# High and low part of an activation in one TensorE product of 512 columns, in two layers of a feed-forward block

## The reference

```python
h = layernorm(x) * (1 + ca) + sa
x = x + ga * attn(h)      # chunked linear attention with a decayed state, 4 heads of 64, chunks of 64 tokens
h = layernorm(x) * (1 + cb) + sb
# feed-forward, ternary weights (-1, 0, 1), a scale for each output
h = silu((h @ w1.T) * s1) * ((h @ w2.T) * s2)     # 256 -> 1024, twice ("l1")
h = gelu((h @ h1.T) * s_h1)                       # 1024 -> 1024 ("l2")
h = gelu((h @ h2.T) * s_h2)                       # 1024 -> 1024 ("l3")
x = x + gb * ((h @ w3.T) * s3)                    # 1024 -> 256 ("y")
```

## Time and profile before

| | |
|---|---|
| median of 3 runs | 1745.33 us (1743.48 to 1747.3) |
| profiled execution, span from first to last instruction | 1742.3 us |
| mean granted TensorE clock | 0.991 of full speed |
| PE / PEld busy | 1716.0 us (98%) / 1651.6 us (95%) |
| DVE / ACT / POOL busy | 1115.4 us (64%) / 963.3 us (55%) / 593.5 us (34%) |

### The profile page before, as it was taken

How to read it: one execution, slowest core, us unless ns; L and a number is a source line. 1 busy time by engine, 2 the same in 40 slices (tenths; PEclk the granted TensorE clock), 3 DMA queues, 4 the chain that set the end, 5 groups by cost and what they waited for, 6 DMA issues and landing times.

```text
span 1742.3 us, 60528 instructions
## 1 busy us (share of the span) xinstructions
PE 1716.0 (98%) x25488; PEld 1651.6 (95%) x25488; DVE 1115.4 (64%) x3041; ACT 963.3 (55%) x2249; POOL 593.5 (34%) x694
## 2 busy tenths in 40 slices
PE   8799999999999999999999999999999999999999
PEld 5698999999999999999999999999999999999998
DVE  5677666666666666676666676666666666666432
ACT  4664555555555555555555555555555555565554
POOL 3544333343333343333243333243233243243101
PEclk8899999999999999999999999999999999999999
DMA  8101000000000000000000000000000000000000
GB/s 291 68 14 33 12 23 23 18 20 11 24 23 23 18 20 11 24 23 24 17 21 15 20 23 23 20 17 19 16 23 23 21 17 21 14 23 17 8 3 12
DMA packets 37356, 47.08 MB, mean 27 GB/s; under 512 B 9236, under 2 KB 29336, under 8 KB 37080
## 3 DMA queue, kind: packets, MB, share of 16 engines
q1 hardware_dynamic: 35088, 40.75, 8.4%
q10 hardware_dynamic: 1992, 2.38, 0.5%
HBM read 22.53 MB, written 8.39 MB: 18 GB/s over the span
## 4 chain that ended last, share of the span: by engine, by line
PE 93%; DVE 1%; issue 1%; POOL 1%; ACT 1%; DVEq 0%; POOLq 0%
PE mlp L1163 64%; PE mlp L1235 6%; PE solo L1163 3%; PE duo L1431 3%; PE solo L1304 3%; PE solo L1136 2%; PE duo L1352 1%; PE duo L1129 1%; PE duo L1420 1%; PE solo L1440 1%; PE duo L1124 1%; PE duo L1325 1%; PE solo L1146 1%; PE duo L1422 1%; PE duo L1316 1%
## 5 line engine op out<-in xcount | busy, mean ns | idle before, releaser
L1163 PE MATMUL mlp<-act_hi,w_hi 128*128 128x256 f32 x4096 | 968.0, 283 | 1.1 <-POOL act_lo L668 0.6
L1163 PE MATMUL mlp<-act_lo,w_hi 128*128 128x256 f32 x4096 | 945.2, 277 | 0.0
L1163 PEld LDWEIGHTS mlp<-act_hi,w_hi 128*128 128x128 f32 x4096 | 770.1, 188 | 9.8 <-POOL act_lo L668 1.3
L1163 PEld LDWEIGHTS mlp<-act_lo,w_hi 128*128 128x128 f32 x4096 | 770.4, 188 | 0.8
L805 ACT ACTIVATE full<-mlp,scale_sb 128x256 f32<-128x256 f32 x512 | 246.4, 481 | 553.7 <-PE mlp L1163 553.5
L895 DVE TENSOR_TENSOR act_lo<-full,act_hi 128x256 fp32r<-128x256 f32 x512 | 240.2, 469 | 321.7 <-ACT act_hi L806 319.1
L668 POOL TENSOR_TENSOR act_lo<-full,act_hi 128x256 fp32r<-128x256 f32 x256 | 186.6, 735 | 501.9 <-ACT act_hi L795 501.9
L806 ACT ACTIVATE act_hi<-mlp,scale_sb 128x256 fp32r<-128x256 f32 x512 | 242.6, 474 | 0.0
L1163 PE MATMUL mlp<-xh,w_hi 128*128 128x256 f32 x768 | 190.8, 286 | 3.5 <-issue 3.0
L1163 PE MATMUL mlp<-xl,w_hi 128*128 128x256 f32 x768 | 189.8, 282 | 0.0
L607 POOL TENSOR_TENSOR rstd<-ve,minus_half 128x2 f32<-128x2 f32 x64 | 49.1, 768 | 331.7 <-DVE ve L844 331.3
(11 more groups left out here) (179 smaller groups left out, 2679.9 us busy)
## 6 DMA issues: line engine op xcount, KB each, us to landing
w_raw<-in_wts SPq DMA_DIRECT2D x22, 512.0 KB, 5.0
kg<-r SPq DMA_DIRECT2D x64, 126.0 KB
xin<-in_x SPq DMA_DIRECT2D x62, 128.0 KB
out_y<-y SPq DMA_DIRECT2D x62, 128.0 KB, 2.5
step_and_inv<-square_t SPq DMA_DIRECT2D x56, 64.0 KB, 2.0
wmod_sb<-in_wmod ACTq DMA_DIRECT2D x1, 1024.0 KB, 9.1
kg<-last SPq DMA_DIRECT2D x64, 2.0 KB
last<-r SPq DMA_DIRECT2D x64, 2.0 KB, 1.7
```

What stands on the lines that cost most here:

```text
L1163: mm = pe.matmul(dst, *general_ops, start=is_first and i == 0, stop=is_last and i == 1)
```

## The change

In columns 0 to 6 of `l2` and `l3` (`WIDE` = 7, so k < 7) the two matmuls of a block become one of 512 columns: `act_hi` and `act_lo` are now two halves of one tile `act` ([8, 2, 256]), and the product writes the high part's sum into the first half of the bank and the low part's into the second. DVE adds the two halves (a `tensor_reduce` over two elements, output `sums`, which is the tile `gate`), ACT applies Gelu twice to that sum from SBUF, and POOL makes the low part. Column 7 keeps its form: 16 matmuls of 256 columns, Gelu from PSUM, low part on DVE. `full` is now used in turn of three.

```diff
+WIDE = HK - 1
-    act_hi = [sb(f"act_hi{i}", [HK, TOK], F32R) for i in range(2)]
-    act_lo = [sb(f"act_lo{i}", [HK, TOK], F32R) for i in range(2)]
+    act = [sb(f"act{i}", [HK, 2, TOK], F32R) for i in range(2)]
+    act_hi, act_lo = ([t[:, :, z, :] for t in act] for z in range(2))
...
+    def low_done(eng, layer, m, k):
+        if layer == 0:
+            eng.wait_ge(l1_low, nth(m, k))
+        elif k < WIDE:
+            eng.wait_ge(low_pool[layer], nth_wide(m, k))
+        else:
+            eng.wait_ge(low_last[layer], m)
+    def bank_read(eng, layer, m, k):
+        if layer == 0:
+            eng.wait_ge(prod_ready, nth(m, k))
+        elif k < WIDE:
+            eng.wait_ge(l_sum[layer], nth_wide(m, k))
+        else:
+            eng.wait_ge(l_act[layer], nth(m, k))
...
 POOL, in its walk:
+                    if name in ("l2", "l3") and k < WIDE:
+                        pool.wait_ge(l_act[layer], nth(m, k))
+                        pool.tensor_tensor(act_lo[layer % 2][:, k, :], full[k % 3][:], act_hi[layer % 2][:, k, :].bitcast(F32),
+                                           ALU.subtract).then_inc(low_pool[layer], 1)
...
 ACT, l2 and l3:
-                        act.wait_ge(l_full[layer], nth(m, k))
-                        if k >= 2:
-                            act.wait_ge(l_ready[layer], nth(m, k - 2))
-                        else:
-                            act.wait_ge(l_ready[layer - 1], nth(m, HK - 2 + k))
-                        act.activation(full[k % 2][:], mlp[k % 2][:, 0:TOK], ACT.Gelu, scale=s)
-                        act.activation(act_hi[layer % 2][:, k, :], mlp[k % 2][:, 0:TOK], ACT.Gelu, scale=s).then_inc(l_act[layer], 1)
+                        if k < WIDE:
+                            act.wait_ge(l_sum[layer], nth_wide(m, k))
+                        else:
+                            act.wait_ge(l_full[layer], nth(m, k))
+                        if k >= 3:
+                            low_done(act, layer, m, k - 3)
+                        else:
+                            low_done(act, layer - 1, m, HK - 3 + (k + 1) % 3)
+                        z, s = sums[k % 2][:] if k < WIDE else mlp[k % 2][:, 0:TOK], scale_sb[:, layer + 1, k:k + 1]
+                        act.activation(full[k % 3][:], z, ACT.Gelu, scale=s)
+                        act.activation(act_hi[layer % 2][:, k, :], z, ACT.Gelu, scale=s).then_inc(l_act[layer], 1)
...
 DVE, l2 and l3:
-                        dve.wait_ge(l_act[layer], nth(m, k))
-                        low_part(layer, k)
+                        if k == WIDE:
+                            dve.wait_ge(l_act[layer], nth(m, k))
+                            low_part(layer, k)
+                        else:
+                            dve.wait_ge(l_full[layer], nth(m, k))
+                            if k >= 2:
+                                dve.wait_ge(l_act[layer], nth(m, k - 2))
+                            elif layer == 2:
+                                dve.wait_ge(l_act[1], nth(m, WIDE - 1 - k))
+                            dve.tensor_reduce(sums[k % 2][:], mlp[k % 2][:].rearrange("p (z t) -> p t z", z=2), AX.X, ALU.add).then_inc(l_sum[layer], 1)
...
 PE, l2 and l3 (and the same helpers in y):
-                            pe.wait_ge(prod_ready if i == 1 else l_act[i - 1], nth(m, HK - 2 + k))
+                            bank_read(pe, i - 1, m, HK - 2 + k)
                         if k >= 2:
-                            pe.wait_ge(l_act[i], nth(m, k - 2))
+                            bank_read(pe, i, m, k - 2)
...
                         for j in range(HK):
                             if k == 0:
-                                pe.wait_ge(l_ready[i - 1], nth(m, j))
-                            mm = product(bank[:, 0:TOK], (w_hi[:, w + j, :], w_full[:, j, :]), (hi[:, j, :], lo[:, j, :]), j == 0, j == HK - 1)
+                                low_done(pe, i - 1, m, j)
+                            if k < WIDE:
+                                ops = (w_full[:, j, :], both[:, j].bitcast(F32)) if general else (w_hi[:, w + j, :], both[:, j])
+                                mm = pe.matmul(bank[:].rearrange("p (z t) -> p z t", z=2), *ops, start=j == 0, stop=j == HK - 1)
+                            else:
+                                mm = product(bank[:, 0:TOK], (w_hi[:, w + j, :], w_full[:, j, :]), (hi[:, j, :], lo[:, j, :]), j == 0, j == HK - 1)
```

More of the change, by code:

```diff
@@ L437, in main, with terms_done, nth_wide @@
     gated = [mlp[0], mlp[1], solo[0]]
+    sums = gate
     def nth(n, k):
         return HK * n - (HK - 1 - k)
+    def terms_done(now, i):
+        return 2 * (FS - 1) * now - (2 * (FS - 1) - i)
+    def nth_wide(n, k):
+        return WIDE * n - (WIDE - 1 - k)
+    def low_done(eng, layer, m, k):
[12 more added lines that the diff above has]
+            eng.wait_ge(l_act[layer], nth(m, k))
     blocks = [(q, c, e) for q in range(NP) for c, e in ((0, 0), (1, 1), (0, 1), (1, 0))]
@@ L894, in low_part @@
                 def low_part(layer, k):
-                    dve.tensor_tensor(act_lo[layer % 2][:, k, :], full[k % 2][:], act_hi[layer % 2][:, k, :].bitcast(F32),
-                                      ALU.subtract).then_inc(l_ready[layer], 1)
+                    dve.tensor_tensor(act_lo[layer % 2][:, k, :], full[k % 3][:], act_hi[layer % 2][:, k, :].bitcast(F32),
+                                      ALU.subtract).then_inc(low_last[layer], 1)
                 def part(name, k, a, p):
@@ L950, in part @@
                             dve.wait_ge(sub_ready[j - 1], now)
-                            dve.stream_shuffle(sub_row[:], sub[:], [i // SB * SB + j for i in range(HB)]).then_inc(term_ready[j - 1], 1)
-                            dve.wait_ge(term_ready[j - 1], 2 * now - 1)
-                            dve.tensor_tensor(sub_term[:], sub_row[:], low[:, :, j:j + 1].to_broadcast([P, 2 * NP, SB]), ALU.mult).then_inc(term_ready[j - 1], 1)
-                            dve.wait_ge(term_ready[j - 1], 2 * now)
+                            dve.stream_shuffle(sub_row[:], sub[:], [i // SB * SB + j for i in range(HB)]).then_inc(term_ready, 1)
+                            dve.wait_ge(term_ready, terms_done(now, 2 * j - 1))
+                            dve.tensor_tensor(sub_term[:], sub_row[:], low[:, :, j:j + 1].to_broadcast([P, 2 * NP, SB]), ALU.mult).then_inc(term_ready, 1)
+                            dve.wait_ge(term_ready, terms_done(now, 2 * j))
                             dve.tensor_tensor(sub[:], sub[:], sub_term[:], ALU.subtract).then_inc(sub_ready[j], 1)
@@ L1180, in layer @@
                         if k >= 3:
-                            pe.wait_ge(prod_ready, nth(n, k - 3))
+                            bank_read(pe, 0, n, k - 3)
                         if general:
```

19 lines of the change are left out of this document (10 added, 9 removed).

## The result

The changed kernel takes **1881.16 us** (median of 4 runs, 1879.9 to 1886.36) against 1745.06 for the kernel before beside it: a ratio of **1.0783, 95% interval 1.0765 to 1.0801**. It is 7.8% slower. The forecast was 1836, slower with a chance of 0.83; the time lies inside the range of 1740 to 1945, and 11 us above the 1810 to 1870 that the prediction gave the forecast itself.

A forecast was written before the change was run, and what follows sets the result against it. PE, busy 98% of the span, was taken as the bound. +3.9 - 0.65 = +3.2 us over 29 steps gives 93, other columns save 2: +91 on 1742.3 is 1833, median 3 higher, 1836; range 1740 to 1945.

The forecast's parts named there:

- rival 3: DVE's sum costs 1.11 us like the strided row, every round 0.42 longer: 1900 us, 1940 with more of POOL; chance 0.17.
- The wide product: PE's 512-column matmul in `l2` and `l3` takes 0.2155 us, saving 11 ns a pair, 40 us over 3584 pairs.
- step for the second layer: In `l2` DVE has room between columns, sums cost nothing there, and seven wide columns save 0.65 us a step.
- The sum: DVE's reduce of 512 PSUM elements takes 0.69 us; as a later heading, the step total of +3.2 us.
- rivals 3 and 4: The second of these: DVE's sum costs 2.57 us by its outputs, DVE bounds, 2100 us or more; chance 0.02.
- The chain through the third layer: Sums queue on DVE behind `norm2`, `intra`, `u`, `fs`; `y` begins 2.6 us later, its second half 3.9.
- The round: DVE's sum 0.62 plus `fs` 1.54, plus about 0.5 held by POOL's low part: 2.66 us against PE's column of 1.72.
- rival 2: POOL's low part does not hold `fs` in the third layer: rounds of 2.16, +1.75 us a step, 1795 us; chance 0.14.
- Waits elsewhere: PE waits before columns 4 to 7 of `l3` and in `y`, none in `l2`.
- Gelu out of SBUF: ACT's Gelu reading the sum from SBUF costs the same as from PSUM, 0.47 us, within 0.05 either way.
- Rival 1: Sums reach PE on time, DVE's third-layer round at most 1.72 us: faster, 1705 us; chance 0.13.
- Rival 5: PE gains nothing from 512 columns: 1876 us, or 1855 with only `l2`'s 19 us lost; chance within the forecast's 0.50.

The follow-up runs named there:

- e4: Changed kernel with POOL's low parts of columns 0 to 6 cut to 32 of 256 tokens from the fourth step on: 1830.07 us, ratio 1.0484.
- e6: Wide product, sum and POOL's low part only in the second layer, the third as in the kernel before: 1762.41 us, ratio 1.0093.
- e10: Changed kernel with `fs` and `expand` moved out of the third layer into the next first layer: 1917.4 us, ratio 1.0978.
- e2: Changed kernel without DVE's sum, ACT reading the high half from PSUM; wide products and POOL's low parts stay: 1768.18 us, ratio 1.0125.
- e9: Changed kernel with the second part of `ln2` on ACT moved behind the Gelus of the third layer's last column: 1865.06 us, ratio 1.0681.
- e11: Changed kernel with `fs` 1 to 3 one column later, `expand` behind `fs` 3, `ln2`'s second part behind column 7: 1833.18 us, ratio 1.0495.
- after: The changed kernel itself, against the kernel before: 1881.16 us, ratio 1.0783.

## Why the prediction was right, and where it was off

The time came out 45 us above the forecast, 136 us lost where 91 were predicted. The direction, the place (the third layer and `y`) and the mechanism were right: sums late in DVE's queue, longer rounds by POOL's hold, ACT's queue before the second half. The size was a third too small, outside the 1810 to 1870 of the forecast itself. That the time still lies in the whole range is owed to rival 3, a sum that costs 1.11, for which the range was drawn up to 1945 and which is not what happened. Step by step:

- **The wide product** (0.2155, bounds 0.2133 to 0.2268): **the term that failed.** It measures 0.233, outside the bounds. The forecast's argument was that the 6.7 ns lost at 256 columns are fixed or shrink with longer streams, by analogy with fp32 products that stream 213 ns a load. Proportion to columns was taken as the worst case, and the truth is worse: 20 ns are lost at 512. Its step for the second layer said -0.65 us; +0.25 was measured.
- **The sum** (0.69, bounds 0.42 to 2.57): 0.686. It was taken at the rate of contiguous elements against the stride row's 1.112, and rivals 3 and 4 fall with it.
- **The chain through the third layer.** From the end of sum 1, the forecast had sums 2 to 6 end 4.0, 6.0, 8.7, 11.3 and 14.0 later, and `y` begin 14.1 later; measured are 3.9, 6.4, 9.1, 11.8, 14.5 and 14.6. The 0.4 to 0.5 between them enter at one place: L967 of `fs` 0 was held too, 0.63 instead of 0.17. Sum 1 itself came as much earlier in the step. The two errors cancel, which is luck. So `y` begins +2.66 (forecast +2.6), its second half +3.92 (forecast +3.9).
- **The round**: 2.70 against 2.66, the hold 0.54 against 0.5. e4 takes the hold away and finds a round of 2.22 and 1830; rival 2 had 2.16 and 1795, the distance being again mostly the product's price.
- **Waits elsewhere.** None in the second layer, as said; e6 shows it. No wait stands before columns 4 and 5 in the step shown (32 wide products run through from 977.62): column 5 begins behind column 4 without one, since a wide column takes PE 1.87 us of its own time, where the forecast had 1.72, and sum 1 came 0.4 earlier than forecast.
- **Gelu out of SBUF**: 0.51 and 0.49 where 0.47 was, within the 0.05 given. `ln2` holds ACT for 1.15 from start to start (991.98 to 993.13), as forecast; its own length is 1.27.
- **Not foreseen**: the second half of `y` takes 0.18 more a step. Its products come 0.118 apart, not 0.1134 (0.08), and the first spacing behind the wait is 0.22 (0.1).
- **The sum.** A step costs +4.35, not +3.2: 0.9 from the second layer's sign, 0.18 from `y`, and the rest is rounding. The 27 steps between the ends carry 123 us (27 x 4.35, and 5 in single longer steps). The step out of `third` costs 7.0, where 3.2 was put down; the start until the first `y` costs 3.7, and the last three steps 2.5, where the ends were forecast as a gain of 2. What makes the ends dearer was not taken apart by a run.
- **The rivals.** Rival 1 (the covers hold) is what e10 shows for the third layer alone. Its condition was a DVE round of 1.72 or less beside that layer, and it fails by `fs`, as forecast. Nearest in time is rival 3, 1900, but its mechanism is not there: sums take 0.686. Rival 5 (PE gains nothing), 1855, has the right sign of the error; PE gained less than nothing.

## What to carry to other kernels

Before a buffer is handed to another engine to free, write out that engine's queue at that point: here the products' bank moved from ACT, which ran ahead, to DVE, which was full in one of three layers, and 113 of 136 us hang on the sum that frees it (e2), 51 of them on POOL's hold of DVE (e4). Order within a queue was worth 48 us (e9 and e11) with no work changed, and moving work off DVE to POOL cost DVE 0.54 us in each round of `fs`, where a two-input instruction met POOL's. Price one wide instruction against the narrow ones it replaces by itself first: a block of 32 would have shown that this one had nothing to give.

## What the runs showed of the hardware that was not expected

- fp32r products cost 0.1134 us at 256 columns, 0.1734 at 384 and 0.2334 at 512, that is 0.469 ns for each further column at a granted clock of 1.00, and 0.110 at 128, only 3.4 ns below 256. fp32 products of 512 columns cost 0.4291 a record in the same run.
- A DVE reduce over pairs that lie 256 values apart in PSUM costs 0.686 us for 512 inputs and 256 outputs, no more than the reduce of 512 contiguous elements in SBUF to 8 outputs. The 1.112 of the reduce at a stride of 8 in SBUF belongs to that row's access, not to its number of outputs.
- Products of 256 columns have two speeds, 0.1134 and 0.118. The slower one is not tied to waits or to wide products: one `y` of the kernel before, from 1644 us on, has it (1.65 and 2.12 in the columns of the table), and in e11 the products of `y` behind its last wait come every 0.1134. What chooses between them was not tested.
- Behind a wait the second product comes some 0.1 us late: 0.22 after the first, in column 7 and in `y`, where the next ones are 0.118 apart.
- DVE can stand still for 2.5 to 2.7 us in the middle of its work with nothing in the profile that it waits for (1551.84 in after, 1491.24 in e6), and PE then waits for it.
